# Signature stage: the first row tile's totals carried in row 0 of the second tile's operand

## The reference, cut to what matters

```python
def step(levels, v):
    e = [v]
    for k in range(1, d):                      # d = 4
        e.append(_outer(e[-1], v) / (k + 1))
    new = []
    for k in range(d):
        acc = levels[k] + e[k]
        for i in range(k):
            acc = acc + _outer(levels[i], e[k - 1 - i])
        new.append(acc)
    sig = jnp.concatenate(new, axis=-1)
    return (tuple(new), sig)
_, sigs = jax.lax.scan(step, init, dx)
return sigs @ W.T + b                          # 8+64+512+4096 numbers per token to 128
```

## Time and profile before

| what | value |
|---|---|
| median of 3 runs | 1924.67 us (1922.48 to 1925.3) |
| profiled execution | span 1922.3 us; the profile gives no time of its own beside it |
| PE, busy | 1656.3 us, 86% of the span |
| DVE, busy | 1402.0 us, 73% |
| ACT, busy | 938.9 us, 49% |
| POOL, busy | 882.1 us, 46% |
| mean granted TensorE clock | 0.942 |

### The profile page before, as it was taken

One profiled execution on the slowest core, in us unless ns is written; L12 is line 12 of the kernel. 1 busy time (PEld: TensorE's weight loads), 2 busy tenths in 40 slices (PEclk: granted clock), 3 DMA queues, 4 the chain that ended last, 5 costly groups with the idle time before them and its releaser, 6 DMA issues. The chain is left out here.

```text
span 1922.3 us, 59270 instructions
## 1 busy us (share of the span) xinstructions
PE 1656.3 (86%) x21927; PEld 1392.3 (72%) x21927; DVE 1402.0 (73%) x3369; ACT 938.9 (49%) x2305; POOL 882.1 (46%) x1710
## 2 busy tenths in 40 slices
PE   5999999999979884999599999999999999648750
PEld 4888888888858773999478888888888888525430
DVE  6777777877758884666787888888888888635434
ACT  2222212221228770677467777777777777424320
POOL 3333333333202566566232455445555555547771
PEclk9999999999989995999699999999999999869985
DMA  8900000000022001222323333333333333256537
GB/s 298 165 0 0 0 0 0 0 0 0 0 81 102 23 25 55 65 72 65 124 60 63 74 87 78 77 77 78 76 79 80 86 77 78 63 149 171 169 102 271
DMA packets 312667, 147.60 MB, mean 77 GB/s; under 512 B 205238, under 2 KB 291284, under 8 KB 312020
## 3 DMA queue, kind: packets, MB, share of 16 engines
q1 hardware_dynamic: 299876, 118.38, 25.3%
q0 software_dynamic: 12544, 25.91, 3.9%
HBM read 72.03 MB, written 73.37 MB: 76 GB/s over the span
## 5 line engine op out<-in xcount | busy, mean ns | idle before, releaser
L2143 POOL DMA_INDIRECT x_slots<-rel_x,rel_at x128 | 135.5, 1059 | 212.5 <-PE rel_s_ps L1727 186.9
L535 PE MATMUL tok_main_ps<-tok_w_h,tok_feat_h 128*128 128x512 f32 x512 | 205.3, 401 | 0.9 <-DVE tok_feat_low L99 0.9
L1966 ACT ACTIVATE rel_e<-rel_s_ps,rel_neg_max 128x255 f32<-128x255 f32 x512 | 200.2, 482 | 10.7 <-DVE rel_neg_max L2299 9.5
L535 PE MATMUL tok_main_ps<-tok_w_h,tok_feat_l 128*128 128x512 f32 x512 | 200.6, 392 | 0.0
L535 PE MATMUL tok_main_ps<-tok_w_l,tok_feat_h 128*128 128x512 f32 x512 | 200.3, 391 | 0.0
L2299 DVE TENSOR_REDUCE rel_neg_max<-rel_s_ps 128x4 f32<-128x1020 f32 x128 | 155.9, 1218 | 53.2 <-PE rel_s_ps L1727 51.2
L84 POOL TENSOR_TENSOR tok_q_pre<-tok_v_q,tok_v 128x128 f32 (+1 forms) x32 | 39.0, 1219 | 310.5 <-DVE tok_q L274 295.8
L1707 PE MATMUL rel_s_ps<-rel_k_h,rel_q_head_h 128*128 128x256 f32 x512 | 154.6, 302 | 0.2 <-DVE rel_q_head_l L2273 0.2
L1748 PE MATMUL rel_t_ps<-all_k_ident,rel_e 128*128 128x128 f32 x1024 | 139.3, 279 | 14.4 <-issue 14.0
L294 DVE TENSOR_TENSOR tok_prod<-tok_main_ps,tok_v 128x1024 f32<-128x1024 f32 x64 | 78.4, 1225 | 97.9 <-PE tok_main_ps L540 97.9
L1748 PEld LDWEIGHTS rel_t_ps<-all_k_ident,rel_e 128*128 128x128 f32 x1024 | 109.6, 141 | 47.0 <-issue 45.8
(11 more groups left out here) (406 smaller groups left out, 4725.2 us busy)
## 6 DMA issues: line engine op xcount, KB each, us to landing
rel_q_rep<-q_rows SPq DMA_DIRECT2D x256, 64.0 KB, 2.5
o_rows<-rel_rv SPq DMA_DIRECT2D x256, 64.0 KB
x_slots<-early_zeros SPq DMA_DIRECT2D x16, 520.0 KB, 6.2
exp_x<-x_slots SPq DMA_DIRECT2D x32, 260.0 KB, 3.0
y_rows<-early_zeros SPq DMA_DIRECT2D x16, 512.0 KB, 5.8
final_y<-y_rows SPq DMA_DIRECT2D x16, 512.0 KB, 12.0
exp_x<-x_slots SPq DMA_DIRECT2D x72, 65.0 KB, 1.9
q_rows<-rel_qT SPq DMA_DIRECT2D x64, 64.0 KB
```

What stands on the lines that cost most here:

```text
L535: nc.tensor.matmul(main_ps[s][:, cols], feat[fk][:, s, j, :], w_p[wk][:, j, cols], start=(j == 0 and (fk, wk) == (0, 0)), stop=False)
L1966: last = nc.scalar.activation(e[u % 2][:, n, 0:L], s_ps[u % 2][:, n, 0:L], ACT.Exp, bias=neg_max[u % 2][:, n:n + 1])
L2143: nc.gpsimd.indirect_dma_start(x1_slots[:], bass.IndirectOffsetOnAxis(ap=at[n][:, k, t:t + 1], axis=0), x1[n][:, t, k, :], None).then_inc( ...
```

## The change

Each row tile now has 127 tokens in rows 1 to 127. Row 0 of tile 0 is empty (its increment is zero), row 0 of tile 1 holds the last token. The tables are remade so that this order comes out right: column 0 of `after` sums rows 1 to 127, and `accumulate(b, 0)` therefore leaves the total of tile 0 in row 0 of `a3`. ACT's new `carry` writes that row over row 0 of the rounded operand of tile 1, DVE's new `carry_remainder` does so for the remainder, and row 0 of the operand matrix `after_r` is all ones, so that the total reaches every row of tile 1. `accumulate(b, 1)` waits for both and makes two products in place of four. `running_sum` turns the order back: four 128 x 128 matrices (`upto`, now 128 x 512) times two operands, eight products of 128 columns in place of two of 256 and two of 128. x is laid out on the host in the new order and loaded in four pieces in place of six; a memset of `v` is gone.

```diff
-                for s, lo, hi in PARTS:
-                    sp.dma_start(x0[lo:hi, s, :], x_t[s * P + lo:s * P + hi, :]).then_inc(x_in, 16)
-                    sp.dma_start(x1[lo:hi, s, :], x_t[s * P + lo + 1:s * P + hi + 1, :]).then_inc(x_in, 16)
+                for s in range(2):
+                    for to, at in ((x0, 0), (x1, T)):
+                        sp.dma_start(to[:, s, :], x_t[at + s * P:at + s * P + P, :]).then_inc(x_in, 16)
...
-                link(nc.vector.memset(v[:], 0.0))
...
-                nc.vector.tensor_copy(after_r[:], after[:])
                 nc.vector.tensor_copy(upto_r[:], upto[:])
+                link(nc.vector.tensor_copy(after_r[:], after[:, 0:P]))
+                nc.vector.tensor_copy(after_r[0:1, :], after[0:1, P:T])
...
+                def carry_remainder(b):
+                    dve.wait_ge(carry_round, b + 1)
+                    rest(nc.vector, r2v_p[1][0:1, 1, :], a3[0:1, 0, :], r2v_p[0][0:1, 1, :])\
+                        .then_inc(carry_rest, 1)
...
                     total(b + 1, 0)
+                    carry_remainder(b + 1)
                     combine(b, 0)
...
+                def carry(b):
+                    act.wait_ge(sum_ready, 2 * b + 1)
+                    nc.scalar.activation(r2v_p[0][0:1, 1, :], a3[0:1, 0, :], ACT.Copy)\
+                        .then_inc(carry_round, 1)
...
                     increments(b - 1)
+                    carry(b + 1)
                     evacuate(b + 1, 0)
...
+                    if s == 1:
+                        pe.wait_ge(carry_rest, b + 1)
                     for k in range(2):
-                        if s == 1:
-                            nc.tensor.matmul(to, after_r[:, P:T], r2v_p[k][:, 0, :], start=(k == 0), stop=False)
-                        last = nc.tensor.matmul(to, after_r[:, 0:P], r2v_p[k][:, s, :],
-                                                start=(k == 0 and s == 0), stop=(k == 1))
+                        last = nc.tensor.matmul(to, after_r[:], r2v_p[k][:, s, :], start=(k == 0), stop=(k == 1))
...
-                    both = h_ps.rearrange("p s d -> p (s d)")
                     for k in range(2):
-                        nc.tensor.matmul(both, upto_r[:, 0:P], inc_p[k][:].rearrange("p s d -> p (s d)"), start=(k == 0),
-                                         stop=False)
-                    for k in range(2):
-                        last = nc.tensor.matmul(h_ps[:, 1, :], upto_r[:, P:T], inc_p[k][:, 0, :], start=False,
-                                                stop=(k == 1))
+                        for s in range(2):
+                            for half in range(2):
+                                part = 2 * s + half
+                                last = nc.tensor.matmul(h_ps[:, s, :], upto_r[:, part * P:(part + 1) * P],
+                                                        inc_p[k][:, half, :], start=(k == 0 and part == 0),
+                                                        stop=(k == 1 and half == 1), skip_group_check=True)
...
-        "upto": (col >= p).astype(f),
+        "after": np.concatenate([(p >= 1) & ((m < 1) | (p < m)), np.ones((P, P), bool)], 1),
+        "upto": np.concatenate([(p >= 1) & (p <= m + 1), (p == 1) & (m == P - 1), np.ones((P, P), bool),
+                                ((p >= 1) & (p <= m + 2)) | ((p < 1) & (m >= P - 2))], 1),
```

More of the change, by code:

```diff
@@ L139, in signature_tokens @@
     TURN = P // 4
-    EVEN = ROWS[1] // 16 * 16
-    PARTS = ((0, 0, P), (1, 0, EVEN), (1, EVEN, ROWS[1]))
-    XS = 16 * (2 * len(PARTS) + 1)
+    XS = 16 * 5
     after, upto, ident = K["after"], K["upto"], K["ident"]
@@ L165, in signature_tokens @@
         w_low_h, w_low_p = (m.sb(f"w_low_{k}", [P, 2, C * D], FP32R) for k in "hp")
-        after_r = m.sb("after_r", [P, T], FP32R)
+        after_r = m.sb("after_r", [P, P], FP32R)
         bias = m.sb("bias", [P, D])
@@ L171, in signature_tokens @@
         inc_p = [m.sb(f"inc_{k}", [P, 2, D], FP32R) for k in "hl"]
-        upto_r = m.sb("upto_r", [P, T], FP32R)
+        upto_r = m.sb("upto_r", [P, 4 * P], FP32R)
         a3_ps = m.ps("a3_ps", [P, 2, NA, P])
@@ L194, in signature_tokens @@
         inc_round, inc_rest = m.sem("inc_round"), m.sem("inc_rest")
+        carry_round, carry_rest = m.sem("carry_round"), m.sem("carry_rest")
         with nc.Block() as block:
@@ L224, in _ @@
                 for s in range(2):
-                    n = ROWS[s]
                     nc.vector.tensor_tensor(
-                        v[0:n, :, s, 1:C],
-                        x1[0:n, s, :].rearrange("p (b c) -> p b c", c=CIN),
-                        x0[0:n, s, :].rearrange("p (b c) -> p b c", c=CIN), ALU.subtract)
+                        v[:, :, s, 1:C],
+                        x1[:, s, :].rearrange("p (b c) -> p b c", c=CIN),
+                        x0[:, s, :].rearrange("p (b c) -> p b c", c=CIN), ALU.subtract)
                     link(nc.vector.tensor_copy(v[:, :, s, 0:1],
@@ L333, in _ @@
                 total(0, 0)
+                carry_remainder(0)
                 total(0, 1)
@@ L347, in _ @@
                 total(1, 0)
+                carry_remainder(1)
                 combine(0, 0, first=True)
@@ L355, in _ @@
                 total(2, 0)
+                carry_remainder(2)
                 combine(1, 0)
@@ L374, in _ @@
                 total(B - 2, 0)
+                carry_remainder(B - 2)
                 combine(B - 3, 0)
@@ L383, in _ @@
                 total(B - 1, 0)
+                carry_remainder(B - 1)
                 combine(B - 2, 0)
@@ L460, in _ @@
                 nc.scalar.activation(w_low_h[:], w[:, NA:NA + 2, :], ACT.Copy).then_inc(w_round, 1)
+                carry(0)
                 evacuate(0, 0, first=True)
@@ L464, in _ @@
                 rounded(1)
+                carry(1)
                 evacuate(1, 0)
@@ L468, in _ @@
                 increments(0)
+                carry(2)
                 evacuate(2, 0)
@@ L477, in _ @@
                 increments(B - 3)
+                carry(B - 1)
                 evacuate(B - 1, 0)
@@ L2920, in shape_tables @@
     p, col = np.arange(P)[:, None], np.arange(T)[None, :]
-    after = (col > p).astype(f)
+    m = col[:, 0:P]
     real = np.ones((P, NT), f)
@@ L2928, in shape_tables @@
     inc = {
-        "after": after,
-        "upto": (col >= p).astype(f),
+        "after": np.concatenate([(p >= 1) & ((m < 1) | (p < m)), np.ones((P, P), bool)], 1),
+        "upto": np.concatenate([(p >= 1) & (p <= m + 1), (p == 1) & (m == P - 1), np.ones((P, P), bool),
+                                ((p >= 1) & (p <= m + 2)) | ((p < 1) & (m >= P - 2))], 1),
         "ident": np.eye(P, dtype=f),
         "one": np.ones((P, 1), f),
-        "after_b": after[:, :P],
+        "after_b": m > p,
         "ones_b": np.ones((P, P), f),
@@ L2963, in layouts @@
     w_low[P + LOWS:P + 3 * P // 4] = 0
+    x_t = a["x"].transpose(1, 0, 2).reshape(T, B * CIN)
+    at = np.r_[0, 0:P - 1, L - 1, P - 1:L - 1]
     query = np.arange(P // HD)[:, None, None] % QUAD
@@ L2970, in layouts @@
     lay = {
-        "x_t": a["x"].transpose(1, 0, 2).reshape(T, B * CIN),
+        "x_t": np.concatenate([x_t[at], x_t[at + (np.arange(T) > 0)]]),
         "w_main": level(NLOW, W.shape[1]),
@@ L2997, in layouts @@
     t = np.diff(np.linspace(0.0, 1.0, T, dtype=np.float32))
-    lay["step_time"] = np.stack([t[:P], np.concatenate([t[P:], np.zeros(P - ROWS[1], np.float32)])], 1)
+    lay["step_time"] = (t[at] * (np.arange(T) > 0)).reshape(2, P).T
     return {n: np.ascontiguousarray(v) for n, v in lay.items()}
```

## The result

The changed kernel takes 1930.94 us (median of 8 runs, 1926.8 to 1936.37) against 1924.99 us before (8 runs), ratio 1.0040 with a 95% interval of 1.0025 to 1.0055. Two more sets of runs, `changed_again` and `changed_third`, gave 1.0034 (1.0016 to 1.0053) and 1.0028 (1.0014 to 1.0043). The medians lie 6.0, 5.6 and 4.7 us apart, and the ratios stand for 7.7, 6.5 and 5.4 us. It is slower, by some 6 us, where I had forecast 2 and called no visible difference the likeliest. The median of 1930.94 us lies at the upper edge of my range of 1920.5 to 1931; the ratio on the 1924.7 us that I started from gives 1932.4, just above it. The profiled execution has a span of 1927.5 us and took 1929.24 us.

A forecast was written before the change was run, and what follows sets the result against it. PE's instruction queue was taken to bound the signature loop, serial chains the start-up and end. -14.5 + 14.7 + 2.4 - 0.5 = +2.1 us on 1924.7 gave 1926.8 us, range 1920.5 to 1931.

The forecast's parts named there:

- the gain taken for the start: Start-up: two DMA issues less give 0.9 us, the larger `upto` load takes 0.3, so the start moves 0.6 us forward.
- the 0.3 us for `turn(0,0)`: Start-up: `turn(0,0)`, queued behind `accumulate(0,1)` on PE, delays the first `evacuate`; up to 0.6 us possible, 0.3 taken.
- an end counted at the full clock: Last `running_sum`, on the chain to the next stage: its four more steps were counted within the 32 sequences at 0.46 us.
- Saved 0.47 and added 0.46 us an iteration: Loop on PE: two `accumulate` products removed save 14.5 us in all; eight `running_sum` products for four add 14.7 us.
- Rival 1: `running_sum`: small products step at 0.06 to 0.09 us, giving 14 to 6 us off, 1913 to 1921 us; chance 0.08.
- Rival 2: Loop: the carry comes late, 0.1 to 0.3 us an iteration, giving 1930 to 1936 us; chance 0.08.
- Its upper bound: Loop: carry and remainder at 1024-column prices, 1.06 and 1.23 us, end at 304.8, 0.3 us late, 9 us in all.
- 2.7 us for the chain: Start-up: from `total(0,0)` through the uncovered first carry to the end of `total(0,1)`, 4.0 us in place of 1.3.
- -0.5 us for a shorter slow stretch: After PE's start-up restart: a later restart changes the half-clock stretch, worth -3 to +1 us; -0.5 taken.
- the rest: Remaining outcomes, such as later stages shifting against their DMAs by some us either way; chance 0.04.
- Case 4: Whole kernel: both halves worth nothing, start-up hidden too, 1924 to 1925 us; chance 0.70 together with the forecast.
- Rival 3: Start-up dearer by another 2 to 4 us, as PE idles more and the slow clock spreads; 1929 to 1931 us; chance 0.10.

The follow-up runs named there:

- changed_again: The changed kernel run a second time against the kernel before: 1932.24 us against 1926.68, ratio 1.0034.
- changed_third: The changed kernel run a third time against the kernel before: 1927.54 us against 1922.88, ratio 1.0028.
- two_more_512: Kernel before with two more 512-column products of a zero matrix in every `accumulate(b,1)`: 1940.3 us in one run, against 1924.65.
- four_more_128: Kernel before with four more 128-column products of a zero matrix in every `running_sum`: 1946.46 us in one run, against 1924.65.
- before_again: The kernel before, unchanged, run as its own rival: 1923.86 us against 1924.65, ratio 0.9996.
- idle_semaphores: Kernel before with two more semaphores in the signature stage that nothing uses: 1921.88 us against 1924.65, ratio 0.9992.
- padded_3: Kernel before with three more small straight-code instructions each on DVE, ACT and PE, moving later code: 1924.29 us against 1922.88, ratio 1.0004.
- pe_wait_alone: Kernel before with one more PE wait, which never holds, in front of `accumulate(b,1)` except for sequence 0: 1924.62 us against 1923.62, ratio 1.0006.
- wide_table: Kernel before with table `upto` made 512 columns wide, its second half unused: 1925.35 us against 1926.68, ratio 1.0000.
- x_in_four: Kernel before with x loaded in four pieces in place of six and no memset of `v`: 1922.46 us against 1923.62, ratio 0.9996.
- first_as_before: Changed kernel with sequence 0 accumulated as before, without carry; against the kernel before: 1929.83 us, ratio 1.0022; again 1925.78 us, ratio 1.0010.

## Why the prediction was wrong, step by step

In short: the stage cost 1.5 us more than its sum said, through the gain taken for the start, the 0.3 us for `turn(0,0)` and an end counted at the full clock. What stands behind the stage, 1 to 4 us of the timed difference, was put at nothing, and its cause stays open.

**The loop: right.** Saved 0.47 and added 0.46 us an iteration was forecast; `two_more_512` and `four_more_128` measure 0.46 for both, and the iteration went from 16.37 to 16.35 us. Rival 1 (small products step faster) is refuted: the measured step is 0.11 to 0.12 us. The 0.06 us of the earlier trace rows that spoke for it came with a next step of 0.12, so that pair took 0.18 us and not two full steps, as I had written; the ladder of weight loads decides. The Trainium skill, TensorE: Matmul & The Clock Gate, section Back-to-back issue gap, gives a sustained 81 ns for 128 columns, and the steps measured here do not agree with it. Rival 2 (the carry is late) is refuted: PE doesn't wait in 400 us. (Its upper bound adds up to 304.69, 0.2 us late, and not to 304.8.)

**The start-up: the mechanism right, the size too small.** I forecast 2.7 us for the chain plus 0.3 for `turn(0,0)`. The slow pace in this chain was read rightly from the 0.63 us of a product at 22.13 (0.39 in the loop), but that is the third start of six and not the last, and the earlier trace rows begin only at 30.50. The chain up to the second `total` took its price: it starts 15.9 us after PE's first product before (24.06 plus one L286 of 0.6, less 8.72) and 18.7 us now (26.66 less 7.95), 2.8 more. A term that failed is the 0.3: `turn(0,0)` cost 0.9 in the first pair of traces and 0.7 on the mean of the three traces of the changed kernel against five with the start-up of before (before, `before_again`, `idle_semaphores`, `padded_3` and `pe_wait_alone`). I had named a bound of 0.6 and taken half. Two things add up in it. The transposes stand behind `accumulate(0,1)`, and DVE had only one L99 of 1.2 us to do meanwhile. And they ran at the slow pace, 0.21 us apart, in all three traces of the changed kernel. In those of before it differs: in `pe_wait_alone` they ran at that pace too, and DVE waited 0.38 us with no carry at all.

The gain from two issues less failed as well. It was 0.77 us in this trace, but PE's first product starts anywhere from 7.78 to 9.18 us in these traces, and over the three of the changed kernel it is only about 0.2 us earlier (8.32 against 8.51 in those five). I had taken 0.6.

**The clock behind the restart: not shown.** I took -0.5 us for a shorter slow stretch, and 4.2 us in place of 6 fits that in the first pair of traces. But that was luck: PE stays at 1.2 GHz for 4.2, 4.3 and 5.0 us behind the restart in the three traces of the changed kernel, and for 6.1, 6.2, 2.9, 3.4 and 4.7 us in those five, 4.5 against 4.6 on the mean. From the restart to PE's last L540 the changed kernel takes 518.5 us and the five take 519.1; most of these 0.6 us are the 0.013 us or more by which each of the 31 iterations is shorter.

**The end: a term at the wrong clock.** I counted four more steps at the full clock there, 0.46 us, and put them into the 32. But PE has been idle for 4.2 us and may run at 1.2 GHz, where each of the four costs 0.21 us. From PE's last L540 to the stage end it is 8.0 to 8.3 us in the three traces of the changed kernel and 7.1 to 7.5 us in the five: 0.9 us, 0.4 more than counted.

**The sum of the stage.** Over the three traces of the changed kernel the stage ends at 564.86, 565.89 and 564.90 us, 565.2 on the mean; over those five 561.6. That is 3.6 us, where I had 2.1.

| part of the stage | forecast, us | measured, three traces against five |
|---|---|---|
| PE's first product earlier | -0.6 | -0.2 |
| chain of the first carry | +2.7 | +2.8 |
| `turn(0,0)` behind it, to the restart | +0.3 | +0.7 |
| restart to the last `main`: loop and clock | -0.8 | -0.6 |
| last `running_sum` to the stage end | +0.5 | +0.9 |
| sum | +2.1 | +3.6 |

**Behind the stage: not forecast, and not settled.** The step of the prediction is "What follows is unchanged work that starts later by the sum." The three sets of timed runs give 5 to 8 us, the stage 3.6, so 1 to 4 us stand behind it by the middle of each set. I had put nothing into the sum for it, and a chance of 0.04 on "the rest". The stage alone would be a ratio of 1.0019: the interval of the first set (1.0025 to 1.0055) leaves it out, those of the other two hold it. The traces do not show the surplus. From the stage end to the end of the span it is 1362.6, 1359.5 and 1359.2 us in the three of the changed kernel, and 1358.4 to 1362.3 in the five, 1360.4 against 1360.3 on the mean; but the three profiled executions were also 1.6 to 5.0 us faster than the medians of their sets. The semaphores are not the cause (1.0001 at most). The wide table and a move of the later code by three instructions, each alone, showed nothing (ratios 1.0000 and 1.0004), though their intervals reach 1.0016 and 1.0018 and so leave room for 3 us.

In six traces of kernels whose signature loops have the instructions of before, the relative attention stage takes 775.1 to 777.6 us; in the ten whose loops have others, 777.7 to 784.6, whether they carry or not. The six are before, `before_again`, `idle_semaphores`, `wide_table`, `x_in_four` and `padded_3`. The pattern was found after the runs, over single executions with several us of scatter in each group; 0.1 us lies between the groups, two of the three traces of the changed kernel stand at their border, and `pe_wait_alone`, which is in the second group, isn't measurably slower. So it shows no cause. The surplus can also be partly scatter: `first_as_before` came out at 1.0022 once and 1.0010 the other time, with a stage that ended within 0.7 us of before both times.

Case 4, both halves worth nothing, was right for the loop alone. Rival 3, a dearer start-up, comes nearest to what happened, and with 1929 to 1931 it had the time, but by luck: it asked for another 2 to 4 us in the start-up, and up to the restart that was 0.9 us dearer than forecast.

## What to carry to other kernels

Price a matrix product by the distance between starts: where each product has its own weights, a product of 128 or 256 columns costs a weight load's step here (0.11 to 0.12 us at the full clock), so trading one product of 512 columns (0.23 us) for two of 128 gives nothing. A carry that is hidden in the loop still costs its whole chain once, in the start-up, where nothing covers it; cost there also what is queued behind the new wait on each engine, to the end. Keep products few where PE comes back from an idle stretch, since they may run at half the clock: 0.21 us a product in place of 0.11. And before a difference of 1 us between two traces is called an effect, look at the same stretch in several traces of each kernel: the slow stretch behind the restart varied by 3 us between traces of kernels with the same signature loop.

## What the runs showed of the hardware

A copy or a subtraction of one partition takes about as long as one of 128: for 512 columns 0.63 us against 0.60 on ACT, and 0.68 us against 0.69 on DVE. The ACT pair differs in its source, SBUF for the one row and PSUM for the 128. The last `running_sum` comes after 4.2 us without work in every trace. In that of before its four products ran at the full clock, 0.68 us from the first to DVE's next (559.50 to 560.18). In that of `idle_semaphores`, with the same four products, the timeline of PE shows them slower, and DVE's next is at 558.66, 1.12 us. Its granted clock stands behind:

```profile
557.54 0.55 PE L554 MATMUL tok_small_ps<-tok_inc_h,tok_upto_r 128*128 128x256 f32 x1 [4.18 <-issue]
557.89 0.42 PE L554 MATMUL tok_small_ps<-tok_inc_l,tok_upto_r 128*128 128x256 f32 x1
558.11 0.31 PE L557 MATMUL tok_small_ps<-tok_inc_h,tok_upto_r 128*128 128x128 f32 x1
```
```profile
557.50:558.60 1.10, 1.06 (x4) 0.93 (x4) 0.00 (x0) 0.00 (x0) 0.00 (x0) 0.50 0.00 0
```

Whether the clock has fallen by then differs from one execution to the next: in before and `before_again` (0.68 us) it had not, in `idle_semaphores`, `padded_3` and `pe_wait_alone` (1.12 us) it had.
